# Pairs of value steps, six buffers of probabilities, and rotation tables loaded span by span, in a causal attention layer

## What is computed

```python
xn = layernorm(x)                                  # eps 1e-5
q, k, v = split(xn @ w_qkv)                        # 16 heads of 16
q, k = rope(q), rope(k)                            # x * cos + rotated(x) * sin, by position
p = softmax(causal(q @ k.T * 16 ** -0.5))
x = x + (p @ v) @ w_proj + b_proj
xn = layernorm(x)
x = x + sqrt((xn @ cos(theta + theta_noise)) ** 2 + (xn @ sin(phi + phi_noise)) ** 2)
```

## Time and profile before

| | us |
|---|---|
| median of 3 runs | 1975.45 |
| lowest, highest | 1974.7, 1977.72 |
| profiled execution | 1979.04 |
| its span, first to last instruction | 1977.3 |
| PE busy | 1939.0 |
| VectorE busy | 1559.9 |
| ScalarE busy | 1389.1 |
| GpSimd busy | 871.0 |

### The profile page before, as it was taken

One profiled execution on the slowest core, in us unless ns is written; L12 is line 12 of the kernel. 1 busy time (PEld: TensorE's weight loads), 2 busy tenths in 40 slices (PEclk: granted clock), 3 DMA queues, 4 the chain that ended last, 5 costly groups with the idle time before them and its releaser, 6 DMA issues.

```text
span 1977.3 us, 38203 instructions
## 1 busy us (share of the span) xinstructions
PE 1939.0 (98%) x12036; PEld 798.1 (40%) x12036; DVE 1559.9 (79%) x4101; ACT 1389.1 (70%) x2687; POOL 871.0 (44%) x1336
## 2 busy tenths in 40 slices
PE   7999999999999999999999999999999999999998
PEld 4333433334443434343443443434444344433335
DVE  5898789988778787887877878888777877879725
ACT  3466668877676777877767777777767767777883
POOL 4714615443535454633544435553444545431232
PEclk9999999999999999999999999999999999999999
DMA  6301312122121221311222121322212212120131
GB/s 143 97 24 28 121 47 73 39 71 65 52 73 54 74 83 64 105 35 64 61 71 77 57 72 56 104 68 71 72 33 71 68 64 78 51 94 7 49 105 57
DMA packets 130762, 133.30 MB, mean 67 GB/s; under 512 B 29434, under 2 KB 105722, under 8 KB 130554
## 3 DMA queue, kind: packets, MB, share of 16 engines
q1 hardware_dynamic: 127728, 128.29, 21.1%
q10 hardware_dynamic: 2832, 2.56, 0.7%
HBM read 38.49 MB, written 25.68 MB: 32 GB/s over the span
## 4 chain that ended last, share of the span: by engine, by line
PE 87%; ACT 5%; issue 2%; DVE 2%; DMA 2%; POOL 1%; SPq 0%; DVEq 0%; POOLq 0%; ACTq 0%
PE banks L1094 23%; PE banks L1079 23%; PE banks L1057 22%; PE banks L1012 6%; PE banks L1001 6%; ACT probs L1198 3%; PE banks L1039 3%; PE banks L946 2%; DVE chunk_max L1399 1%; PE banks L935 1%; DMA squares<-sums 1%; PE banks L928 1%; PE banks L1065 0%; DVE banks L1394 0%; PE banks L1024 0%
## 5 line engine op out<-in xcount | busy, mean ns | idle before, releaser
L1198 ACT ACTIVATE probs<-banks 128x512 f32<-128x512 f32 (+1 forms) x2240 | 1143.9, 602 | 328.6 <-PE banks L1079 289.3
L1399 DVE TENSOR_REDUCE chunk_max<-banks 128x1 f32<-128x512 f32 x1536 | 985.3, 683 | 216.7 <-PE banks L1057 215.0
L1079 PE MATMUL banks<-queries,stack_k 99*128 99x512 bf16 (+3 forms) x2560 | 740.5, 350 | 11.8 <-ACT probs L1198 4.1
L1057 PE MATMUL banks<-stack_k,queries 96*128 96x512 bf16 (+3 forms) x2560 | 712.2, 349 | 8.2 <-DMA queries<-parts 2.8
L1394 DVE CUSTOM_DVE_ANT_0 banks<-banks,row_mask 128x128 f32<-128x128 f32 (+3 forms) x1024 | 483.7, 508 | 87.4 <-PE banks L1057 86.8
L1094 PE MATMUL banks<-probs,v_one 128*17 128x512 f32 (+3 forms) x5120 | 527.8, 532 | 1.1 <-POOL probs L1526 0.6
L1079 PEld LDWEIGHTS banks<-queries,stack_k 99*128 99x128 bf16 x2560 | 231.4, 97 | 435.9 <-ACT probs L1198 218.7
L1057 PEld LDWEIGHTS banks<-stack_k,queries 96*128 96x128 bf16 x2560 | 233.0, 97 | 310.9 <-DVE chunk_max L1399 67.3
L1526 POOL TENSOR_SCALAR_AFFINE_SELECT probs<-probs 128x512 f32<-128x512 f32 x256 | 160.9, 638 | 402.5 <-ACT probs L1198 402.0
L1094 PEld LDWEIGHTS banks<-probs,v_one 128*17 128x17 f32 x5120 | 119.7, 96 | 266.3 <-issue 173.7
L1394 DVE DVE_READ_ACCUMULATOR2_ANT chunk_max<- 128x1 f32 x1024 | 144.0, 141 | 0.0
(11 more groups left out here) (158 smaller groups left out, 1162.3 us busy)
## 6 DMA issues: line engine op xcount, KB each, us to landing
queries<-parts SPq DMA_DIRECT2D x384, 64.0 KB, 2.6
stack_k<-parts SPq DMA_DIRECT2D x354, 64.0 KB, 2.6
sums<-o_raw SPq DMA_DIRECT2D x64, 256.0 KB, 2.3
rot<-raw SPq DMA_DIRECT2D x236, 64.0 KB, 2.0
xin<-x SPq DMA_DIRECT2D x17, 512.0 KB, 4.2
mid<-x SPq DMA_DIRECT2D x13, 512.0 KB, 5.1
heads_t<-sums SPq DMA_DIRECT2D x26, 256.0 KB
inverse<-inverses SPq DMA_DIRECT2D x26, 256.0 KB
```

The lines of the kernel that those rows point to most:

```text
L1057: mm = nc.tensor.matmul(bank[:, n * wide:(n + 1) * wide], queries[0:SPLIT_ROWS, query_place(u, t), h + n, j * P:(j + 1) * P], stack_k[u % ...
L1079: mm = nc.tensor.matmul(bank[:, a * wide:(a + 1) * wide], stack_k[u % 2][0:ROWS, j // SUB, first + a, (j % SUB) * P:(j % SUB + 1) * P], qu ...
L1198: nc.scalar.activation(probs[:, g % PROBS, first:first + many, w0:SPAN], bank, ACT.Exp).then_inc(s_exp, 1)
L1399: nc.vector.tensor_reduce(to, bank[:, 0:count * wide].rearrange("p (h n) -> p h n", h=count), AX.X, ALU.max).then_inc(s_emptied["DVE"], 1)
```

## The change

Four things change together. The value matmuls of two steps are always one piece of work (`VALUES` 1 to 2). There are six buffers of probabilities instead of five. The two tables of all positions (16 KB in each partition) give way to `turn_t`, two buffers that hold cosines and sines of one span (8 KB), and each of the 64 spans that are rotated loads its own in one DMA of 512 KB, from an input in which the two tables are interleaved by span. And the due times of the plan have other values, so that each engine's order is another. The matmuls themselves, the exponentials and the reductions are the same in number and size.

```diff
-PROBS = 5
+PROBS = 6
...
-VALUES = 1
+VALUES = 2
...
-MAX_LEAD = .578
-QK_LEAD = .737
-EARLY = .545
-X_LEAD = .189
-V_LEAD = .418
-SLACK = .9
-PATIENCE = .008
+MAX_LEAD = 0.63
+QK_LEAD = 0.718
+EARLY = 0.691
+X_LEAD = 0.187
+V_LEAD = 0.325
+SLACK = 1.3
+PATIENCE = 0.012
...
-MAX_FIRST = .033
-HOLD = .763
-STICK = 0
-RUN = 4.358
-TURN_LAG = .725
+MAX_FIRST = 0.036
+HOLD = 0.542
+STICK = 0.001
+RUN = 4.842
+TURN_LAG = 0.76
...
-PACE = .924
+PACE = 0.989
...
-    for c in range(1, SPANS):
-        job(("tables", c), "SP", 0.9, CLOCK[0, c - 1] - 1.05, [("qk", 0, c - 1, KT - 1)], 5.0)
...
+            if i:
+                job(("tables", u, c), "SP", 0.6, at - 0.1, [("qk", *last, KT - 1), *([used] if i > 1 else [])], 4.0)
+            free = [("rope", *last, ROPE_OPS - 1), ("tables", u, c)] if i < ROPE_DVE else [used]
...
-        cos_t = sb("cos_t", [P, SEQ])
-        sin_t = sb("sin_t", [P, SEQ])
+        turn_t = sb("turn_t", [P, 2, 2, SPAN])
...
-                if i < FIRST * SPANS:
-                    engine.wait_ge(s_tables[c], 32)
-                ins = ops.tensor_tensor(turned[:, :], raw[:, i % 2, :], cos_t[:, span], ALU.mult)
+                engine.wait_ge(s_tables[i % 2], 16 * (i // 2 + 1))
+                ins = ops.tensor_tensor(turned[:, :], raw[:, i % 2, :], turn_t[:, i % 2, 0, :], ALU.mult)
...
-                def load_tables(c):
-                    columns = slice(c * SPAN, (c + 1) * SPAN)
-                    sp.dma_start(cos_t[:, columns], cosines[:, columns]).then_inc(s_tables[c], 16)
-                    sp.dma_start(sin_t[:, columns], sines[:, columns]).then_inc(s_tables[c], 16)
+                def load_tables(u, c):
+                    i = PLACE[u, c]
+                    if i - 2 in range(ROPE_DVE):
+                        emptied(sp, ("qr", *PROJECTED[i - 2]))
+                    elif i >= 2:
+                        sp.wait_ge(s_rope, ROPE_OPS * (i - 2) + 2)
+                    sp.dma_start(turn_t[:, i % 2, :, :], rotations[:, c, :, :]).then_inc(s_tables[i % 2], 16)
...
-    return lay(cos), lay(sin), np.eye(P, dtype=np.float32), corner, one
+    return np.stack([lay(cos), lay(sin)], 1).reshape(P, 2, SPANS, SPAN).transpose(0, 2, 1, 3), np.eye(P, dtype=np.float32), corner, one
```

More of the change, by code:

```diff
@@ L292, in plan @@
                 after += [("fetch", *ago), ("fetch_k", *ago)] if n == 3 else []
-                after += [("tables", c)] if n == 0 and c and u == 0 else []
+                after += [("tables", u, c)] if n == 0 else []
                 if i < ROPE_DVE:
@@ L592, in layer_kernel @@
         s_wv = sem("value_weights_loaded")
-        s_tables = [sem(f"rotation_tables_loaded{n}") for n in range(SPANS)]
+        s_tables = [sem(f"rotation_tables_loaded{n}") for n in range(2)]
         s_corner = sem("diagonal_mask_loaded")
@@ L653, in rope @@
             i = PLACE[u, c]
-            span = slice(c * SPAN, (c + 1) * SPAN)
             if i < ROPE_DVE and n == 2:
@@ L1577 @@
     from concourse.bass_utils import run_bass_kernel_spmd
-    cosines, sines, eye, corner, one = tables()
+    rotations, eye, corner, one = tables()
     w = np.asarray(L0_attn_w_qkv)
@@ L1587 @@
         "theta": L0_ffn_theta, "phi": L0_ffn_phi, "theta_noise": L0_ffn_theta_noise, "phi_noise": L0_ffn_phi_noise,
[L1588 removed]
+        "rotations": rotations, "eye": eye, "corner": corner, "one": one,
         "w_last": w_last.reshape(P, DIM),
```

27 lines of the change are left out of this document (12 added, 15 removed).

## The result

The changed kernel takes 2003.4 us (median of four runs, 1999.92 to 2005.61) against 1976.1 us (1974.7 to 1977.72): a ratio of 1.0135, with a 95% interval of 1.0122 to 1.0149. It is slower by 27 us where 7 were forecast, and above the upper end of the range, 1998. The profiled execution took 2005.61 us, its span is 2003.9 us, 26.6 more than before.

What follows compares the result with a forecast made beforehand. PE was taken as the bound, busy 1939.0 of 1977.3 us. Terms: -13.4 + 12 + 5 + 3.6 = +7 us, 1986 for the profiled execution, a median of 1982.5 us; range 1965 to 1998.

Steps and rivals of the forecast that it cites:

- Turns: Switching PE into and out of value matmuls: 302 stretches become 238, 0.21 us each, saving 13.4 us.
- Tail fillers: Filler matmuls behind the last value matmuls: 35 instead of 19, 0.22 us each, adding 3.6 us.
- Streaks of maxima: Runs of 15 and 11 maxima without a score between, where PE waits for VectorE: 5 us more, bounds 0 and 6.
- Close reuses: Banks claimed again before their reader has emptied them: 283 instead of 198, adding 12 us, bounds 0 and about 25.
- The clock: PE's granted clock: read as at its upper level, 2.4 GHz, in every slice; no term in the sum.
- Tables: Rotation tables loaded span by span, 31 MB more: hidden by early rotations and idle GpSimd, so 0 us.
- The sixth buffer: One more buffer of probabilities keeps ScalarE four steps ahead while a pair is summed: 0 us.
- The rival of doubled waits: ScalarE falls more than one exponential behind at close bank reuses: waits of 25 us, sum +21, 1996.5 us; 17%.
- The wash: What PE gains at value-matmul switches it waits for exponentials: sum 0, 1975.5 us; 20%.
- spans that run slower evenly from 300 us on: Sign of a wrong forecast: would speak for ScalarE's queue and not for single bank reuses; no size given.

Runs made afterwards that it cites:

- e2: The kernel before with VALUES = 2 (pairs) and nothing else, old due times, five buffers, both tables resident: 2005.1 us, ratio 1.0122.
- e1: The changed kernel with VALUES = 1 (single value steps) again, its due times, six buffers and tables by span kept: 1984.1 us, ratio 1.002.
- f1: The changed kernel, pairs kept, with another set of due times chosen for few close bank reuses: 1992.3 us, ratio 1.0076.
- i1: The changed kernel with VALUES = 4, four steps always together: 2060.6 us, ratio 1.0411.
- h3: The kernel before with only the fillers' due times searched anew for few close bank reuses: 1973.3 us, ratio 0.9988.
- g1: e1 with useless matmuls ahead of maxima, from the sixth on, in the two long streaks: 1983.4 us, ratio 1.0027.
- e3: The changed kernel with VALUES = 1, five buffers and all old due times, so only tables loaded span by span are left: 1977.6 us, ratio 0.9998.
- e4: The changed kernel with table loads after the first two cut to 16 of 512 columns, result partly wrong: 1999.3 us, ratio 1.0095.
- f2: e1 with table loads after the first two spans cut to 16 columns, result partly wrong: 1972.6 us, ratio 0.9973.
- j1: The changed kernel with exponentials from step 24 on covering only 128 columns of each bank, result partly wrong: 1974.5 us, ratio 0.9985.
- j2: The kernel before with exponentials from step 24 on covering only 128 columns of each bank, result partly wrong: 1956.7 us, ratio 0.9892.

## Why the prediction failed, step by step

- **Turns: right.** -13.4 was forecast from 64 stretches of 0.21 us; the starts give -13.7, and the turn is unchanged in the rows above.
- **Tail fillers: right.** 3.6 forecast, 3.5 measured. The tail as a whole, from the end of the last values (1952.65 us), is 51.2 us instead of the 48.5 I named, because the chain holds 7.1 us of the output projection behind them and 3.5 before, where I had seen 0.87 move; that is work which counts in both.
- **Streaks of maxima: right in size.** 5 forecast. The streaks of 11 and 15 lose 4.8 and 4.1 us, the old one of 8 lost 2.5: +6.4. The old one stands at 44.6 to 48.0 us in the trace, and not at 68 to 74 us as I said: there scores stand among the maxima, and the rows show VectorE's pace only the earlier trace rows. What the streaks do to the clock was left out.
- **Close reuses: the step that failed.** It said +12, with bounds 0 and 25. The waits are +27 in all, of which the streaks are 6.4, so some 20 are left. "I take 12, since the sum by single reuses met the row to 0.01 us": one row met it, at a place where ScalarE was free when the bank filled. The sum over the kernel did not. The count gave 22 us for the kernel before, whose trace already held 52.1 us of waits ahead of scores and maxima: I never laid the one beside the other. The table shows how steady that ratio is: 2.4 before, 2.2 after, 2.5 for e2, 2.6 for e1, 2.4 for f1, 2.2 for i1 and for h3. Scaled by the 2.4 of the kernel before, the 12 us would have been 28, near the +27 of all waits; the 20 that are left stood inside my bounds, and with the clock the sum did not. The factor of two was on record before all of these runs, and the times came out above what it gave each time (e1 by 10 us, e2 by 13, f1 by 8, i1 by 26, h3 by 1); the 2.2 to 2.6 were formed afterwards. Why the ratio is so steady has not been taken apart beyond the two causes shown: a queue ahead of the reader (862 us) and a reader that first stood idle during a pair (1904 us). In the changed kernel, exponentials that stood behind other work of ScalarE account for 27.8 us of lost time ahead of scores (13.9 before), those that started at once for 15.6 (10.3), and maxima that waited for VectorE for 23.4 (13.4).
- **The clock: a term that was put at nothing.** I read "upper level in every slice" as no term at all. The page's 40 slices are 50 us wide and hid the 10.2 us before as well as the 30.7 us after, which is +10 us at most. In e1 and h3 one wait of PE of 2.7 us went with 10.2 us at 1.2 GHz, which loses another 5 us, so that it cost nearly three times itself; in g1 a wait of 2.96 us went with 3.4 us at that level.
- **Tables: right alone, wrong together.** 0 was forecast, and e3 confirms it for the old due times (0.9998). Together with the change's due times the loads are worth 4 us with pairs (e4) and 11.5 us with single steps (f2). The sentence that failed is that a span's rotation is read tens of us before PE needs it: in e1 a late swap reached PE by way of GpSimd's and ScalarE's queues and not by the rotated keys.
- **The sixth buffer: not tried by itself.** Pairs with five buffers (e2) take 2005.1 us and with six (the changed kernel) 2003.4, under different due times. ScalarE's idle time ahead of exponentials that value matmuls ended is 33.2 us in e2 and 15.2 in the changed kernel (29.4 before), so the buffer may ease that wait, and what it is worth in time is open.

The rival of doubled waits (1996.5) was nearest in mechanism: its waits are 31 us against the 27 measured, and with the clock's 10 us, which it lacked too, it would have given 2006.5. The wash named ScalarE's length as the bound of a stretch. The rows at 1889 us show that bound for the kernel before, where ScalarE runs without a pause; with pairs it isn't even reached. The Trainium skill (TensorEngine Tiling (Array Packing), PSUM Bottleneck) says that emptying PSUM may become the bottleneck once tiling has quickened TensorE. This case agrees in part: j1 and j2 move the difference from 27 to 17.8 us by halving the time of the exponentials alone. Of spans that run slower evenly from 300 us on, the prediction said that they would speak for ScalarE's queue and not for single reuses. They came: counted by stretches of 300 us, the waits from 300 us on grow by about half, in all but one of the six stretches, and 862 and 1904 to 1921 us are far from the streaks.

Where the profile of e1 shows loads ahead of a swap, the Trainium skill (DMA: Bandwidth & Descriptors, Queues, rings and completion order) says that descriptors of a queue are taken in order on each DMA engine. The 5.54 us for which GpSimd waited on four swaps, whose median from issue to landing is 2.0 us in the changed kernel, agrees.

## What to carry to other kernels

Before a count of single losses is used for a difference, lay its sum for the kernel before against the waits that the trace of before shows; if the trace has 2.4 times as much, the difference has to be scaled or the missing cause found, and even scaled by two it fell short here each time. Longer pieces on the bounding engine save its switching cost but empty and then jam the few buffers between it and its readers: with four banks and exponentials of 0.5 to 0.6 us, a piece of 1.7 us was already too long. Read the granted clock in windows of some us around every long wait, since it doesn't show in the page's slices, and ask which engine sets the pace there before half of the stretch is booked as lost.

## What the runs showed of the hardware

The granted clock fell to 1.2 GHz 0.7 us before the end of one wait of PE of 2.70 us (h3) and 0.6 us before the end of one of 2.73 us (e1), and it fell in a streak in which PE had 0.22 us of work in every 0.60 us. It stayed low for 10.2, 10.2 and 6.8 us, with PE busy for 8.9, 9.6 and 6.6 us of them. A wait of 2.96 us in g1 went with 3.4 us at that level, so the length of the wait alone did not set how long the clock stayed low. A load of ScalarE's function tables took 1.28 us, and the activation behind it started 0.01 us after its end. The Trainium skill (ScalarE: Activation LUTs, What ACT_TABLE_LOAD costs) gives 1283 ns for the load, which agrees, and about 1380 ns more for a drain at each switch, which the rows at 305 to 309 us do not show.
